# A decoder layer on one core: setup split in fourths, cross keys and values moved in among the transposes, statistics of the next batch taken four steps later

## What is computed

```
x = x + attention1(layernorm(x))      # 16 heads, softmax over 64 random features, keys and queries apart
x = x + attention2(layernorm(x), ctx) # 8 heads, 77 context rows; k = ctx @ Wk + bk, v = ctx @ Wv + bv
x = x + experts(layernorm(x))         # causal attention, 8 heads x 8 experts, one expert chosen per head and row
```

## Time and profile before

| | |
|---|---|
| median of 3 runs | 1012.2 us (1009.75 to 1013.5) |
| the profiled execution | 1008.53 us, its span 1006.7 us |
| PE busy | 946.7 us (94%) |
| DVE busy | 684.6 us (68%) |
| ACT busy | 392.1 us (39%) |
| POOL busy | 239.2 us (24%) |

### The profile page before, as it was taken

How to read it: one execution, slowest core, us unless ns; L and a number is a source line. 1 busy time by engine, 2 the same in 40 slices (tenths; PEclk the granted TensorE clock), 3 DMA queues, 4 the chain that set the end, 5 groups by cost and what they waited for, 6 DMA issues and landing times.

```text
span 1006.7 us, 14712 instructions
## 1 busy us (share of the span) xinstructions
PE 946.7 (94%) x5620; PEld 734.5 (73%) x5620; DVE 684.6 (68%) x1051; ACT 392.1 (39%) x683; POOL 239.2 (24%) x261
## 2 busy tenths in 40 slices
PE   5879989999999999989999899999999999999997
PEld 3448868888755565689996687788876666659997
DVE  2555757546656778788876675665575767879786
ACT  5424556312266557510104346540204755761000
POOL 6211324123433214145610013220012201311000
PEclk9988999999999999999999999999999999999999
DMA  6112100252135430235541000012221000023663
GB/s 226 29 42 74 53 1 2 70 175 83 55 126 207 145 130 23 73 109 168 174 143 68 1 1 1 2 49 84 84 84 42 23 21 1 22 74 88 195 191 103
DMA packets 33848, 81.56 MB, mean 81 GB/s; under 512 B 5956, under 2 KB 10660, under 8 KB 33780
## 3 DMA queue, kind: packets, MB, share of 16 engines
q1 hardware_dynamic: 32500, 76.44, 23.4%
q10 hardware_dynamic: 1280, 4.20, 1.6%
HBM read 61.26 MB, written 19.20 MB: 80 GB/s over the span
## 4 chain that ended last, share of the span: by engine, by line
PE 73%; DVE 11%; ACT 4%; issue 4%; DMA 3%; POOL 2%; SPq 2%; ACTq 0%; DVEq 0%; POOLq 0%
PE ps L1054 17%; PE ps L1352 10%; PE ps L1289 6%; PE ps L1357 5%; PE ps L1204 4%; PE ps L1249 4%; DVE region L948 3%; PE ps L1062 3%; PE ps L1265 3%; PE ps L1156 3%; PE ps L1218 3%; PE ps L1171 2%; PE ps L1325 2%; PE ps L1326 2%; SPq L303 2%
## 5 line engine op out<-in xcount | busy, mean ns | idle before, releaser
L1289 PE MATMUL ps<-region 128*128 128x512 f32 (+3 forms) x384 | 161.4, 504 | 0.0
L927 DVE TENSOR_REDUCE region<-ps 128x1 f32<-128x512 f32 (+1 forms) x192 | 98.1, 550 | 65.7 <-PE ps L1268 65.7
L715 ACT ACTIVATE region<-ps 128x512 f32<-128x512 f32 x192 | 92.3, 487 | 125.1 <-PE ps L1328 113.6
L972 DVE COPY_PREDICATED region<-region,ps 128x512 f32<-128x512 uint32 x112 | 82.0, 736 | 71.9 <-PE ps L1054 71.3
L1352 PE MATMUL ps<-expert_hi,kst 128*128 128x256 f32 x512 | 126.1, 284 | 3.5 <-DVE kst L1002 2.5
L1352 PE MATMUL ps<-expert_lo,kst 128*128 128x256 f32 x512 | 124.4, 281 | 0.0
L1054 PE MATMUL ps<-expert_hi,wide_hi 128*128 128x512 f32 x256 | 102.6, 401 | 0.0
L1352 PEld LDWEIGHTS ps<-expert_hi,kst 128*128 128x128 f32 x512 | 97.2, 190 | 4.5 <-DVE kst L1002 2.9
L1054 PE MATMUL ps<-expert_hi,wide_lo 128*128 128x512 f32 x256 | 100.0, 391 | 0.0
L1054 PE MATMUL ps<-expert_lo,wide_hi 128*128 128x512 f32 x256 | 99.8, 390 | 0.0
L519 ACT ACTIVATE region<-ps 64x512 f32<-64x512 f32 (+4 forms) x146 | 80.9, 557 | 47.1 <-PE ps L1171 20.0
(11 more groups left out here) (143 smaller groups left out, 1797.0 us busy)
## 6 DMA issues: line engine op xcount, KB each, us to landing
region<-hot_rows SPq DMA_DIRECT2D x128, 128.0 KB, 3.4
expert_hi<-halves_kept SPq DMA_DIRECT2D x24, 512.0 KB, 3.7
expert_lo<-halves_kept SPq DMA_DIRECT2D x24, 512.0 KB, 4.8
halves_kept<-expert_hi SPq DMA_DIRECT2D x16, 512.0 KB, 2.7
halves_kept<-expert_lo SPq DMA_DIRECT2D x16, 512.0 KB, 3.9
expert<-in_value_experts SPq DMA_DIRECT2D x8, 512.0 KB, 5.0
expert<-in_output_experts SPq DMA_DIRECT2D x8, 512.0 KB, 5.1
gb<-gate_rows ACTq DMA_DIRECT2D x16, 256.0 KB, 3.8
```

The lines of the kernel that those rows point to most:

```text
L715: act.activation(PT[:, g % RING, lo:CH], ps[:, 4 + g % 2, 0:CH - lo], ACT.Exp).then_inc(sem["pt_ready"], 1)
L927: dve.tensor_reduce(mx[:, i, at_mx:at_mx + 1], ps[:, max_bank(h, m), 0:w], AX.X, ALU.max).then_inc(sem["s_max"], 1)
L972: dve.copy_predicated(V3_heads[:, t], chosen.unsqueeze(3).broadcast_to([P, PAIRS3, 2, HD3]), ps[:, n % 4, :].rearrange("p (a i k) -> p a i ...
L1289: mm(ps[:, SUM_BANK[c], lo:CH], V3[:, j, h // 2, h % 2 * HD3:(h % 2 + 2) * HD3], PT[:, g % RING, lo:CH], start=(j == 0), stop=(j == TC * ( ...
```

## The change

X of batch 0 comes in four loads with a semaphore each; the order of the later loads changes, `WkT` gets a semaphore of its own, and `W3q` is loaded early. In the setup POOL makes scale and shift for two tiles at once (`rstd_of_two`, four operations), the buffers `mv`, `ve`, `rstd`, `shift` are four deep in every layernorm, and DVE applies tiles 5 to 7 (`BY_SCALAR`). Context values and keys are made between the transposes, in banks 6 and 7 of PSUM; `kblk` is written in two groups of 8 in the key phase, ahead of the first query projection. `v2` lies in the region where the last tile of `E1` will be, so that tile's write waits for `v2_placed`; 12 DMAs that carry both batches replace the 24. `W3_hi` is made at t = 0 and 4. The join of the row maxima becomes a reduce with a single input. The statistics, their application and the transposes of the second batch come four steps later.

```diff
-        v2 = expert[0:SKV, 0:B * H2 * V2W].rearrange("p (b h w) -> p b h w", b=B, h=H2)
         bv2 = view(D)
         neg_f = view(2 * P).rearrange("p (i s) -> p i s", i=2)
+        at[0] = (TT - 1) * H1 * NF
+        v2 = view(B * H2 * V2W)[0:SKV].rearrange("p (b h w) -> p b h w", b=B, h=H2)
...
-        STATS_AT = {3 * t + 2: t for t in range(TT)}
-        APPLY_AT = {3 * t + 4: t for t in range(TT)}
-        TURN_AT = {3 * t + 5: t for t in range(TT)}
+        STATS_AT = {3 * t + 6: t for t in range(TT)}
+        APPLY_AT = {3 * t + 8: t for t in range(TT)}
+        TURN_AT = {3 * t + 9: t for t in range(TT)}
...
-            sp.dma_start(X[:, 0, 0:TC, :], xv[0, :, 0:TC, :]).then_inc(x_first, 16)
-            sp.dma_start(const[:, :], d["const"]).then_inc(const_in, 16)
-            sp.dma_start(X[:, 0, TC:TT, :], xv[0, :, TC:TT, :]).then_inc(x_second, 16)
+            for i in range(TT // 2):
+                sp.dma_start(X[:, 0, 2 * i:2 * i + 2, :], xv[0, :, 2 * i:2 * i + 2, :]).then_inc(x_in[i], 16)
+                if i == 0:
+                    sp.dma_start(const[:, :], d["const"]).then_inc(const_in, 16)
+            for w, n in ((W2k, "W2k"), (W2v, "W2v"), (ctxT, "ctxT")):
+                sp.dma_start(w, d[n]).then_inc(kv_in, 16)
+            sp.dma_start(WkT[:, :, :], d["WkT"]).then_inc(wk_in, 16)
+            sp.dma_start(cols[:, :], d["cols"]).then_inc(cols_in, 16)
+            for w, n in ((bv2, "bv2"), (neg_f, "neg_f")):
+                sp.dma_start(w, d[n]).then_inc(side_in, 16)
             sp.dma_start(rows[:, :, :], d["rows"]).then_inc(rows_in, 16)
-            for w, n in ((W2k, "W2k"), (W2v, "W2v"), (ctxT, "ctxT"), (bv2, "bv2"), (neg_f, "neg_f")):
-                sp.dma_start(w, d[n]).then_inc(kv_in, 16)
-            sp.dma_start(cols[:, :], d["cols"]).then_inc(cols_in, 16)
-            for w, n in ((WkT, "WkT"), (WqT, "WqT"), (WvT, "WvT"), (W0, "W0")):
+            for w, n in ((W0, "W0"), (WvT, "WvT"), (WqT, "WqT")):
                 sp.dma_start(w[:, :, :], d[n]).then_inc(front_in, 16)
             for w, n in ((WoT, "WoT"), (W2q, "W2q"), (W2o, "W2o"), (Wg, "Wg")):
                 sp.dma_start(w[:, :, :], d[n]).then_inc(later_in, 16)
+            sp.dma_start(expert[:, :], d["W3q"]).then_inc(w3_in, 16)
             sp.dma_start(X[:, 1, :, :], xv[1]).then_inc(x_next, 16)
 
             sp.wait_ge(blocks_clear, 2)
             sp.wait_ge(c2v_sb, B)
-            for bb in range(B):
-                for h, r0, r1, c in V2_RUNS:
-                    w0 = (h - FIRST2[c]) * V2W
-                    sp.dma_start(vblk[r0 - c * P:r1 - c * P, bb, c, w0:w0 + V2W],
-                                 v2[r0 - h * SKV:r1 - h * SKV, bb, h, :]).then_inc(v2_placed, 16)
-
-
-            sp.wait_ge(v2_placed, 16 * B * len(V2_RUNS))
-            sp.dma_start(expert[:, :], d["W3q"]).then_inc(w3_in, 16)
+            for h, r0, r1, c in V2_RUNS:
+                w0 = (h - FIRST2[c]) * V2W
+                sp.dma_start(vblk[r0 - c * P:r1 - c * P, :, c, w0:w0 + V2W],
+                             v2[r0 - h * SKV:r1 - h * SKV, :, h, :]).then_inc(v2_placed, 16)
+
             sp.wait_ge(w3_lo, 1)
...
+                def rstd_of_two(t):
+
+                    two = slice(t % 4, t % 4 + 2)
+                    until(pool, "var_ready", 0, t + 2)
+                    if t >= 4:
+                        until(pool, "xn_ready", 0, t - 2)
+                    pool.tensor_scalar(ve[:, two, 0], mv[:, two, 1], EPS_LN, None, ALU.add
+                                       ).then_inc(sem["ve_ready"], 2)
+                    until(pool, "ve_ready", 0, t + 2)
+                    pool.tensor_tensor(rstd[:, two, 0], ve[:, two, 0], minus_half.broadcast_to([P, 2]),
+                                       ALU.pow).then_inc(sem["rstd_ready"], 2)
+                    until(pool, "rstd_ready", 0, t + 2)
+                    pool.tensor_tensor(shift[:, two, 0], mv[:, two, 0], rstd[:, two, 0], ALU.mult
+                                       ).then_inc(shift_made, 1)
+                    pool.wait_ge(shift_made, t // 2 + 1)
+                    pool.tensor_scalar(shift[:, two, 0], shift[:, two, 0], -1.0, None, ALU.mult
+                                       ).then_inc(sem["shift_ready"], 2)
+                    until(pool, "shift_ready", 0, t + 2)
+
                 if b == 0:
-                    for t in range(TT):
-                        rstd_of(b, 0, t)
...
-                norm_apply(0, 0, t)
+                if t < BY_SCALAR:
+                    norm_apply(0, 0, t)
...
+            def cross_blocks(bb):
+
+                for a in range(DA):
+                    for h in range(4):
+                        r, col = HD2 * h, (a * B + bb) * SKV
+                        last = act.activation(kblk[r:r + HD2, bb, a, h * SKV:(h + 1) * SKV],
+                                              ps[r:r + HD2, 7, col:col + SKV], ACT.Identity,
+                                              bias=cols[r:r + HD2, 6 + a:7 + a])
+                last.then_inc(c2k_sb, 1)
+
             act.wait_ge(cols_in, 16)
             act.wait_ge(blocks_clear, 2)
...
-                    if b == 0 and t in (2, 6):
+                    if b == 0 and t < B:
+                        cross_blocks(t)
+                    if b == 0 and t in (0, 4):
...
-                    w, at_mx = min(CH, (t + 1) * P - c * CH), t + c * (TT - TC)
+                    w, at_mx = min(CH, (t + 1) * P - c * CH), t if t < TC else t + TC * (c + 1)
...
+            for t in range(BY_SCALAR, TT):
+                until(dve, "shift_ready", 0, t + 1)
+                until(dve, "xn_ready", 0, t)
+                until(dve, "xnT_ps", 0, t - 1)
+                dve.tensor_scalar(xn[:, t % 2, :], X[:, 0, t, :], mv[:, t % 4, 0:1], rstd[:, t % 4, 0:1],
+                                  ALU.subtract, ALU.mult).then_inc(sem["xn_ready"], 1)
...
+                        if b == 0:
+                            dve.wait_ge(v2_placed, 16 * len(V2_RUNS))
...
-                        dve.tensor_tensor(mx[:, i, TC:TT], mx[:, i, TC:TT], mx[:, i, TT:NB], ALU.max
-                                          ).then_inc(sem["tile_max"], 1)
+                        dve.tensor_reduce(mx[:, i, TC:TT], mx[:, i, TT:2 * TT].rearrange("p (c t) -> p t c", c=NC),
+                                          AX.X, ALU.max).then_inc(sem["tile_max"], 1)
...
             pe.wait_ge(const_in, 16)
             for t in range(TT):
                 norm_transpose(0, 0, t)
-            cross_keys_values()
-            pe.wait_ge(front_in, 16 * LOADS_FRONT)
+                if t == 2:
+                    pe.wait_ge(kv_in, 16 * LOADS_KV)
+                if 2 <= t < 2 + B:
+                    cross_values(t - 2)
+                if 2 + B <= t < 2 + B + DA:
+                    cross_keys(t - 2 - B)
+            pe.wait_ge(wk_in, 16)
             for b in range(B):
...
-                pe.wait_ge(c2k_sb, B)
-                pe.wait_ge(c2v_sb, B)
+                if b == 0:
+                    pe.wait_ge(c2v_sb, B)
+                    pe.wait_ge(front_in, 16 * LOADS_FRONT)
...
+                        if b + n == 0:
+                            pe.wait_ge(c2k_sb, B)
```

83 lines of the change are left out of this document (38 added, 45 removed).

## The result

| | before | changed |
|---|---|---|
| median of 4 runs | 1011.3 us (1009.75 to 1013.5) | 983.23 us (982.71 to 985.28) |
| the profiled execution, its span | 1008.53 us, 1006.7 us | 985.28 us, 983.5 us |
| PE busy | 946.7 us (94%) | 937.1 us (95%) |

The ratio is 0.9733, with a 95% interval of 0.9712 to 0.9755: the change makes the kernel 25 to 29 us faster. The prediction had 992 us and a range that begins at 985; it gave 0.02 to what came, less than 985.

What follows compares the result with a forecast made beforehand. PE, busy 94% of the span, was taken as the bound; 13.6 (key phase and setup) + 3.1 (row maxima) + 3.1 (output steps) = 19.8 us off 1008.53 gives 988.7, plus the kept 3.7 offset 992 us, range 985 to 1001.

Steps and rivals of the forecast that it cites:

- the rivals: Gap follows the call (0.20, about 998); setup and `kblk` give less (0.10, 1000 to 1006); slower (0.03); nothing measurable (0.03).
- the carried offset: Whole kernel: median taken to stay 3.7 us above the profiled execution, turning 988.7 into 992 us.
- the sum of 19.8: Total predicted gain in us: 13.6 key phase and setup, 3.1 row maxima, 3.1 output steps.
- Setup, 4.4: Start of the kernel: first key projection at 18.4 instead of 22.84 us, gain 4.4 us.
- the 10.1 for the third tile: Setup: third tile transposed by about 10.1 us, with PE the bound from there.
- The new stall, 2.5: Key phase: PE waits 2.5 us for ACT's `kblk` before the first query projection, until near 40 us.
- The clock behind it, 1.0: Key phase: PE's lower clock after the new stall costs 1.0 us, between bounds 0 and 1.9.
- Configuration, 6.69 behind `W_lo`: Key phase: POOL is free 6.69 us after the second `W_lo`, so the maximum starts at 57.7 instead of 70.53.
- the sums' own 1.8: Key phase: PE's sums run at full clock after a shorter idle time, gaining 1.8 us.
- Row maxima, 3.1: Join with one SBUF operand: both slow joins fall to about 0.2 us, PE gets back 3.1 us.
- Output steps, 3.1: Batch 0's output steps: the wait for `xn` and slow stretch go, gaining 3.1 us.
- Nothing for the deeper buffers, `v2_placed` and the loads: Deeper buffers and `v2_placed` before the last subtraction cost nothing; moved loads are not late.

Runs made afterwards that it cites:

- e5: The changed kernel, unedited, measured again: median 985.08 us, ratio 0.9751, profiled execution 983.23 us.
- g1: The kernel before, unedited, one further profiled execution: 1004.42 us.
- g2: The kernel before, unedited, one more single profiled execution: 1007.0 us.
- e3: Changed kernel with the context keys and values made behind the last transpose again: 988.84 us, ratio 0.9804.
- e4: Changed kernel with the second rounding of W3 at tile 3 instead of 4: 984.44 us, ratio 0.9749.
- f1: Changed kernel with batch 1's statistics, application and transposes back at their old steps: 987.6 us, ratio 0.9796.
- e2: Changed kernel with the join of the row maxima back as a DVE operation with two SBUF operands: 989.69 us, ratio 0.9802.
- e7: Changed kernel with eleven extra matmuls ahead of the first transpose: 986.1 us, ratio 0.9769.
- g3: Changed kernel with the two-operand join of the row maxima back, a single profiled execution: 989.61 us.
- f4: Kernel before with eleven extra matmuls ahead of its first transpose: 1010.06 us, ratio 1.0009.

## Why the prediction was too high

The waits and overlaps it named are in the traces, at most of the places it gave; none of the rivals happened. What failed is the carried offset, the size of the setup's term, and the clock, which it took to be at the full rate in the setup. Of 8.8 us, the sum has 3.4 (23.2 between the two profiled spans, 19.8 predicted); the offset that was carried over has 3.7; and 2.1 is the changed kernel's profiled execution above its median; rounding took 0.4 off.

- **"The median of the runs shown lies 3.7 above it, which I keep"**: this step failed. e5 shows that the offset belongs to the execution. The two profiled executions of the changed kernel average 984.3, among its medians, while three of the kernel before average 1006.7, under its 1010.1 to 1011.3. Medians give 25 to 28 us, the means of all executions 25.1 (1009.2 of 23, 984.2 of 10), profiles 22.4. The profiles of before flatter it by the fast steps of g1 and g2, 2.3 us in the mean of three, and 22.4 + 2.3 is 24.7, so most of this difference is chance in which executions were profiled. The granted clocks on record say the same of the clock: half rate costs at most 12.7 us in the mean of the 23 and 4.2 in that of the 10, 8.4 apart, where the profiles have 7.1. Against 25.1 the sum of 19.8 is 5.3 too small.
- **Setup, 4.4**: mis-sized. It measured 7.6 in the pair of profiles and 5.8 in the means of all. The working priced the context matmuls and projections at the durations of rows 1 and 2 and took PEclk's 1.00 for them; at 0.34 us a weight load they were half-rate durations, so that "the setup's short gaps left the clock alone" is wrong too. The order of the work, the 10.1 for the third tile and PE as the bound were right.
- **The new stall, 2.5**: right in kind, 2.15 us, ending at 36.6 instead of 40 (3.2 of it the setup's extra gain in this pair).
- **The clock behind it, 1.0**: 1.7 on the chain. From the query projection to `ak_top` 16.80 us passed where batch 1 takes 15.05; in e3, e4 and f1 the same stall left the clock alone and the projection took 1.98 to 1.99, in the first profile, e2, e5, e7 and g3 2.75 to 3.28. So it differs between executions; the three are those whose key features come latest, at 26.2 to 27.0 us against 24.4 to 25.4, and why this goes together no run shows.
- **Configuration, 6.69 behind `W_lo`**: right (6.65), and the sums' own 1.8 came as predicted. The sums stood 1.8 us earlier than forecast, 3.2 from the setup less the clock and smaller terms. The stage gave 10.3 us and not 9.2; the stretch near 90 us that is gone accounts for about 1.7 and was in no term.
- **Row maxima, 3.1**: the waits are gone and the stage gives 3.1 to 3.8, near the prediction; in medians the edit gives 4.6 to 6.6, and the difference stays open.
- **Output steps, 3.1**: 2.7 in the means of the table, 3.5 by f1, right; next late is what was named, DVE's `kst` and pieces of the expert.
- **Nothing for the deeper buffers, `v2_placed` and the loads**: right as far as the rows show, but for f1, where PE waits 0.81 us for the context's load.

What the sum lacked as a whole is the clock: it counted 0.8 us for it in the key phase and some in the output steps, and up to 7.1 are in the traces behind the setup, beside what the half rate costs in the setup itself.

## What to carry to other kernels

Where PE's idle times of 2 us and more are taken away, count a half-rate stretch behind each with a chance, not only the wait (here five in eight, four in seven, and none behind twelve waits of 1.5 us); look which wait the stretch stands behind before it is charged to one; and read PE's rate in the first 30 us from the duration of like weight loads, not from the granted clock. Set a forecast against several executions of the kernel before, carry no offset from a single one, and compare stages that the change doesn't touch first. A one-off configuration on POOL's queue is best brought forward by finishing whatever stands ahead of it earlier; once it is hidden, the next bound decides what that is worth (PE in e4).

## What the runs showed of the hardware

- PEclk reads 1.00 in the first microseconds of the trace while the weight loads show the half rate (the kernel before, until 26). In f4, whose PE starts at 2.20, the same stretch reads 0.53. This row is f4's window, the one under it f4's from 17 to 20:

```profile
8.00:16.00 8.00, 3.91 (x13) 1.67 (x13) 2.53 (x12) 5.32 (x12) 6.38 (x19) 0.53 1.06 358
17.00:20.00 3.00, 2.89 (x11) 2.79 (x12) 0.00 (x0) 0.74 (x4) 2.69 (x5) 0.50 0.57 178
```

- The same wait of PE (2.15 us, same place) was followed by the lower clock in five executions and not in three.
- At a granted clock of 1.00 and with PE busy without a pause, the output steps took 2.72 us in g1 and g2 and 2.80 or 2.83 in the other profiles (the last 23 of the second batch).
- POOL's 6.6 us behind its configuration instruction elapse while it waits for a semaphore (0.2 us from input to start in e4).
